# Two PSUM banks in turn for the row maxima and three for the exponentials, in an attention and FP4 feed-forward kernel

## The reference, cut to what matters

```
xn = layernorm(x)
q = rope((xn @ Wqa @ Wqb).reshape(b, s, 16, 8))
k, v = (xn @ Wkva @ Wkvb).reshape(b, s, 4, 8, 2)[..., 0], [..., 1];  k = rope(k)
scores = einsum('bqhd,bkhd->bhqk', q, k) * 8 ** -0.5, causal
attn = softmax(scores) @ v @ Wout + bout
h = silu(fp4(xn) @ fp4(w_gate).T) * (fp4(xn) @ fp4(w_up).T)
out = x + attn + fp4(h) @ fp4(w_down).T
```

## Time and profile before

| | |
|---|---|
| median of 3 runs | 816.93 us (815.31 to 818.28) |
| the profiled execution, its own time | 814.38 us |
| its span, first to last instruction | 812.6 us |
| busy share of PE, DVE, POOL, ACT | 91%, 78%, 75%, 68% |
| mean granted TensorE clock | 0.985 of full speed |
| DMA, mean | 72 GB/s |

### The profile page before, as it was taken

The page is one execution under the profiler, slowest core; times in us unless marked ns, Lnnn a source line. Parts: engine busy times, 40 slices in busy tenths (PEclk is TensorE's granted clock), DMA queues, the critical chain, the costliest instruction groups (busy, mean ns, idle before and its releaser), DMA issues.

```text
span 812.6 us, 18664 instructions
## 1 busy us (share of the span) xinstructions
PE 742.4 (91%) x6641; PEld 465.3 (57%) x6733; DVE 636.3 (78%) x1394; ACT 554.2 (68%) x1170; POOL 606.1 (75%) x707
## 2 busy tenths in 40 slices
PE   2376999999999999999999999999999999999986
PEld 1233555665656566665656566665656566665544
DVE  5569888888788888888788888888788888877511
ACT  1212677777777777777777777777777777677672
POOL 5533697878788797878788797878788797856662
PEclk9977899999999999999999999999999999999999
DMA  4423232141414233241414232141414232240000
GB/s 113 122 55 103 55 97 59 57 114 47 100 33 111 54 97 73 66 105 46 101 34 110 55 103 68 57 114 46 102 35 107 54 94 63 59 99 3 28 8 20
DMA packets 66518, 58.24 MB, mean 72 GB/s; under 512 B 17554, under 2 KB 56434, under 8 KB 66426
## 3 DMA queue, kind: packets, MB, share of 16 engines
q1 hardware_dynamic: 66426, 57.04, 27.4%
HBM read 31.81 MB, written 18.61 MB: 62 GB/s over the span
## 4 chain that ended last, share of the span: by engine, by line
PE 73%; DVE 8%; ACT 6%; POOL 5%; issue 3%; SPq 2%; DMA 2%; another core or an unknown queue 0%; POOLq 0%; DVEq 0%; ACTq 0%
PE pv_ps L1057 18%; PE max_ps L1021 12%; PE exp_ps L1036 11%; PE misc_ps L1073 6%; PE max_ps L1022 6%; PE misc_ps L1122 5%; DVE neg_max L662 4%; PE misc_ps L1081 3%; PE misc_ps L1100 3%; ACT P L854 2%; PE misc_ps L1120 2%; PE misc_ps L1110 2%; PE misc_ps L1090 1%; POOL P L478 1%; PE misc_ps L1077 1%
## 5 line engine op out<-in xcount | busy, mean ns | idle before, releaser
L662 DVE TENSOR_REDUCE neg_max<-max_ps 128x1 f32<-128x512 f32 (+3 forms) x768 | 433.4, 594 | 110.3 <-PE max_ps L1022 108.7
L854 ACT ACTIVATE P<-exp_ps 128x512 f32<-128x512 f32 x512 | 293.5, 596 | 176.8 <-remote 95.7
L1021 PE MATMUL max_ps<-K,Q 128*128 128x384 bf16 (+2 forms) x768 | 199.7, 279 | 24.6 <-DMA Kd<-K 10.9
L1036 PE MATMUL exp_ps<-Q,K 128*128 128x384 bf16 (+3 forms) x932 | 208.4, 292 | 7.5 <-ACT P L854 6.0
L1022 PE MATMUL max_ps<-Kd,Q 128*128 128x128 bf16 x1024 | 190.7, 221 | 1.5 <-DVE neg_max L662 1.5
L478 POOL TENSOR_SCALAR_AFFINE_SELECT P<-P 128x512 f32<-128x512 f32 x256 | 161.6, 667 | 32.6 <-ACT P L857 32.6
L1057 PE MATMUL pv_ps<-P,V 128*32 128x512 f32 (+3 forms) x2048 | 164.2, 439 | 1.2 <-POOL P L478 0.8
L1021 PEld LDWEIGHTS max_ps<-K,Q 128*128 128x128 bf16 x768 | 75.2, 100 | 96.0 <-DVE neg_max L662 42.7
L1022 PEld LDWEIGHTS max_ps<-Kd,Q 128*128 128x128 bf16 x1024 | 99.4, 99 | 42.6 <-issue 22.8
L510 POOL TENSOR_TENSOR h<-gate_sb,up_half 128x352 f32<-128x352 f32 x64 | 59.6, 932 | 62.4 <-DVE gate_sb L675 62.3
L1036 PEld LDWEIGHTS exp_ps<-Q,K 128*128 128x128 bf16 x1024 | 82.3, 98 | 37.0 <-ACT P L854 14.2
(11 more groups left out here) (113 smaller groups left out, 1024.0 us busy)
## 6 DMA issues: line engine op xcount, KB each, us to landing
Q<-q_scr SPq DMA_DIRECT2D x64, 224.0 KB
q_scr<-q_split SPq DMA_DIRECT2D x16, 384.0 KB, 2.6
Kd<-K SPq DMA_DIRECT2D x64, 96.0 KB
x_in<-x SPq DMA_DIRECT2D x16, 256.0 KB, 5.3
q_scr<-q_split SPq DMA_DIRECT2D x16, 256.0 KB, 2.9
x_res<-x SPq DMA_DIRECT2D x16, 256.0 KB, 5.8
out<-y SPq DMA_DIRECT2D x32, 128.0 KB, 3.1
K<-k_scr SPq DMA_DIRECT2D x64, 48.0 KB
```

The lines of the kernel that those rows point to most:

```text
L662: nc.vector.tensor_reduce(neg_max[:, pr // 4, i, heads[0]:heads[0] + len(heads), pr % 4], max_ps[r % 3][:, 0:len(heads) * n].rearrange("p ...
L854: nc.scalar.activation(P[g % 2][:, hh + r % 2, col:col + 512], ps[:, :], ACT.Exp, scale=SCALE).then_inc(exp_done, 1)
L1021: nc.tensor.matmul(ps[:, col:col + d], Qt, Kt[:, half, g, 0:d], start=True, stop=True)
L1036: last = nc.tensor.matmul(exp_ps[n % 2][:, col:col + width], K[par][:, half, pr // 2, kb * 128:(kb + 1) * 128], Q[par][:, pr, kb * 128:S], ...
```

## The change

One bank moves from the maxima to the exponentials. The maximum tiles use two banks in turn (`r % 2`; there are six tiles per pair, so the turn stays even across pairs) and the wait of PE before tile r is now for the reduction of the tile two places before. The exp tiles use three banks in turn, counted over all batches since 40 tiles per batch is no multiple of three, and the wait of PE before an exp tile is for ACT's reading of the tile three places before. No instruction is added, removed or put elsewhere on any engine.

```diff
-        max_ps = [... (f"max_ps{i}", [128, 512], F32)) for i in range(3)]
-        exp_ps = [... (f"exp_ps{i}", [128, 512], F32)) for i in range(2)]
+        max_ps = [... (f"max_ps{i}", [128, 512], F32)) for i in range(2)]
+        exp_ps = [... (f"exp_ps{i}", [128, 512], F32)) for i in range(3)]
...
-                                        max_ps[r % 3][:, 0:len(heads) * n].rearrange("p (h k) -> p h k", k=n),
+                                        max_ps[r % 2][:, 0:len(heads) * n].rearrange("p (h k) -> p h k", k=n),
...
-                ps = exp_ps[n % 2]
+                ps = exp_ps[(T.batch(0) * NPAIR * NEXP + n) % 3]
...
-                T.wait(pe, max_read, NPAIR * NMAX, 1, pr * NMAX + r - 2)
+                T.wait(pe, max_read, NPAIR * NMAX, 1, pr * NMAX + r - 1)
...
-                Kt, ps, g, n = K[T.par(1)], max_ps[r % 3], pr // 2, (i + 1) * 128
+                Kt, ps, g, n = K[T.par(1)], max_ps[r % 2], pr // 2, (i + 1) * 128
...
-                T.wait(pe, exp_done, NPAIR * NEXP, 0, n - 1)
+                T.wait(pe, exp_done, NPAIR * NEXP, 0, n - 2)
...
-                    last = nc.tensor.matmul(exp_ps[n % 2][:, col:col + width], ...
+                    last = nc.tensor.matmul(exp_ps[(T.batch(0) * NPAIR * NEXP + n) % 3][:, col:col + width], ...
```

More of the change, by code:

```diff
@@ L218, in build @@
         hqT = sb("hqT", [128, 3, S])
-        max_ps = [ctx.enter_context(nc.psum_tensor(f"max_ps{i}", [128, 512], F32)) for i in range(3)]
-        exp_ps = [ctx.enter_context(nc.psum_tensor(f"exp_ps{i}", [128, 512], F32)) for i in range(2)]
+        max_ps = [ctx.enter_context(nc.psum_tensor(f"max_ps{i}", [128, 512], F32)) for i in range(2)]
+        exp_ps = [ctx.enter_context(nc.psum_tensor(f"exp_ps{i}", [128, 512], F32)) for i in range(3)]
         pv_ps = ctx.enter_context(nc.psum_tensor("pv_ps", [128, 512], F32))
@@ L1035, in exp_tile @@
                     width = S - kb * 128
-                    last = nc.tensor.matmul(exp_ps[n % 2][:, col:col + width], K[par][:, half, pr // 2, kb * 128:(kb + 1) * 128],
+                    last = nc.tensor.matmul(exp_ps[(T.batch(0) * NPAIR * NEXP + n) % 3][:, col:col + width], K[par][:, half, pr // 2, kb * 128:(kb + 1) * 128],
                                             Q[par][:, pr, kb * 128:S], start=True, stop=True)
```

## The result

| | before | after |
|---|---|---|
| median | 816.84 us (815.31 to 818.28, 4 runs) | 842.56 us (841.69 to 844.79, 4 runs) |
| ratio, 95% interval | | 1.032 (1.030 to 1.035) |
| the profiled execution, its own time / span | 814.38 / 812.6 us | 841.69 / 839.9 us |

The change makes the kernel 3.2% slower. 847 was forecast, with 826 to 862 as the range.

A forecast was written before the change was run, and what follows sets the result against it. PE was taken to bound the kernel, its delays paid in 15 full iterations: 31.7 + 2 (iteration -1) - 4 (tail) = +29.7 us on the profiled 814.38, 844.1; with the median 2.55 above that execution, 847 us, range 826 to 862.

The forecast's parts named there:

- What bounds the kernel: Full iterations: PE busy 44.86 of 45.69 us; a PE delay is paid 15 times unless PE stood still later for something fixed.
- six places: Per full iteration, delays in slots 4 (0.89), 7 (0.67), 1 (0.12), 2 (0.16), 5 (0.13) and 6 (0.14 us).
- stricter wait: PE's wait before a maximum tile, now for a reduction one place later; to cost 2.11 us per full iteration.
- 15 times the sum: The 15 iterations with both maxima and exponentials: 2.11 us lost in each, +31.7 us.
- looser wait: PE's wait before an exp tile, now for an ACT reading one place earlier; to gain 0 in the 15 full iterations.
- Iteration -1: Iteration with maxima but no exponentials: +2 us, ends 0 and +5; losses after 62 us hidden under the DMA chain.
- The tail: After the last maxima: third exp bank lets PE reach the product with V earlier; -4 us, ends -1 and -8.
- The granted clock: Full iterations: PE clock to stay 1.00 despite new pauses; rival, a fall to 0.83, about 987 us, chance 0.04.
- They swallow: Rival: new pauses shrink PE's old waits for `o_norm` and `up_half`, leaving 0.87 us per iteration; 828 us, chance 0.10.
- Only the largest: Rival: DVE catches up fully, so an iteration loses only slot 4's 0.89 us; 827 us, chance 0.09.
- They add: Rival: slot 4's shortfalls stand side by side, 3.30 us in place of 0.89; 883 us, chance 0.07.
- Faster: Rival: pauses are covered by queued matmuls, so the tail decides at -4 us; 813 us, chance 0.03.

## Why the prediction was right

- **What bounds the kernel.** Right. In iterations 1 to 13 the PE's delays were paid at every one of the six places, with 0.13 given back behind slot 7 and 0.04 in slot 5, and nothing but the stricter wait was needed for them.
- **The stricter wait, 2.11 us per iteration.** Measured 1.88. Five of the six places came out within 0.02 of the forecast, slot 4 with its give-back among them. The term that was off is slot 7: 0.67 forecast, 0.57 - 0.13 measured. DVE's x_scale had taken 0.27 in the kernel before, where it started while POOL's addition was running, and takes 0.17 now, which is the 0.10. The 0.13 is given back at the transpositions of h and the product with V behind them, which had short gaps of their own; I had let only tile 4 of slot 4 give anything back.
- **15 times the sum, +31.7.** Measured +26.8: 24.4 for 13 iterations, 0.8 for iteration 0 and 1.6 for iteration 14. These two were taken as full, and were not. In iteration 14 it is the term for the looser wait that failed. It was put at 0 for all 15 iterations from waits read between 148 and 676 us, which lie in iterations 1 to 13; in iteration 14 exp tiles did wait for ACT (7 times, 2.2 us). The stricter wait alone costs 2.2 us there (45.10 against 42.89), much as forecast, and the third exp bank gives back 0.65. In the kernel before, iteration 0 has 4 such waits, 1.8 us, that are gone in the changed kernel; there the runs don't separate what each of the two waits does.
- **Iteration -1, +2.** Measured +3.6, within its ends of 0 and +5. I took what comes after 62 us to be hidden under the DMA chain. In the chain of waits of the changed kernel, it is PE and DVE in turn right up to the next iteration:

```profile
79.27 0.70 DVE neg_max L662
...
80.02 0.50 PE max_ps L1021
...
80.66 1.29 DVE neg_max L662 x2
...
83.80 0.70 DVE neg_max L662
...
84.55 0.50 PE max_ps L1021
```

  With three banks the maxima of that iteration were done in time for the PE to wait for DMAs there; with two they end after the DMAs. The step that failed is the overlap: the DMA chain hides nothing once the maxima end behind it.

  The granted clock of this iteration was also lower, 0.75 where it was 0.82, but that is not the 3.6 us: with the stricter wait alone in the kernel before, the clock is 0.84 and the iteration takes 40.9 us all the same. The iteration in the kernel before, in the changed kernel, and with the stricter wait alone:

```profile
43.93:81.21 37.28, 27.87 (x168) 15.05 (x169) 32.87 (x75) 8.90 (x20) 15.07 (x21) 0.82 0.28 74
```
```profile
43.67:84.55 40.88, 30.46 (x168) 15.93 (x169) 33.59 (x75) 8.80 (x20) 15.21 (x21) 0.75 0.25 69
```
```profile
44.14:85.03 40.89, 29.48 (x168) 15.64 (x169) 33.80 (x75) 8.91 (x20) 15.15 (x21) 0.84 0.26 71
```

- **The tail, -4.** Measured -3.0. The third bank saves up to one exponential in most slots, as supposed: by the first exp tile of slot 7 the tail is 3.9 ahead. Then 1.0 is given back at the first transposition of h, which waits for POOL's last quantization step. That step ends at 818.88 + 2.60 = 821.48, and the weight load and the matmul of the transposition follow:

```profile
818.88 2.60 POOL L494 TENSOR_TENSOR h<-h,h_scale 128x1408 f32<-128x1408 f32 x1
...
821.59 0.42 PEld L1100 LDWEIGHTS misc_ps<-ident,h 128*128 128x128 f32 x4 [1.03 <-issue]
...
821.62 0.63 PE L1100 MATMUL misc_ps<-ident,h 128*128 128x128 f32 x4 [0.82 <-POOL h L494]
```

  I had named POOL as what could hold the PE in the tail, and left the size open.
- **The sum.** The parts make +27.3 us on the span of the profiled executions, where +29.7 was forecast. That the difference is so small is in part luck: 4.9 us too much in the iterations 0 to 14 stand against 1.6 too little in iteration -1 and 1.0 too much gain in the tail.
- **The granted clock.** As forecast it stays at 1.00 in iterations 1 to 13, and on to the end of the span, with a pause of 1.1 us in each iteration. The rule named ahead (the Trainium skill, TensorE: Matmul & The Clock Gate, section "A second HAM failure mode: psum-queue depth-cycling") did not come to bear here.
- **The rivals.** "They swallow" is out: from 148 to 676 us the waits for `o_norm` and `up_half` are as long as before (9.9 us in 12 waits and 4.6 in 11, where it was 9.1 in 11 and 4.5 in 11). "Only the largest" is out: all six pauses are there. "They add" is out: slot 4 costs 0.87, not 3.30. "Faster" needed the pauses to be covered by queued matmuls; five of the six moved the matmuls' starts by what was forecast, within 0.02 us, and slot 7 by 0.44. Two of their prices were not worked out like the rest: "only the largest" took the tail at -5 in place of -4, which gave 827 where -4 gives 828, and "faster" left out the +2 of iteration -1 and what slot 4 might cost.

## What to carry to other kernels

How many buffers a ring needs is not told by the consumer's mean rate (DVE was busy 85% of the iteration before) but by the longest stretch of other work between two of its reads: compare, tile by tile, the end of the read two or three places back with the start of the producer, and sum what is negative, giving back only at places where the producer already waits for the same thing. Read it in every phase: here the first and the last iteration of the 15 behaved otherwise than the 13 between them. Where such a stretch is short of a buffer, moving the consumer's other work by a tile or two can be worth most of the buffer (here 20.2 of 25.7 us, though the same move also takes 5.0 us off the kernel that has the buffer). A buffer that pays in one phase can be lent in that phase: a bank idle in the tail gave the 3.0 us that the third exp bank gains there, at no cost.

## What the runs showed of the hardware

The DVE operations `h_mag` and `x_scale`, whose one input lies in SBUF, wait for POOL's operations. `h_mag` (1408 elements) takes 0.52 us alone and 0.99 beside four causal operations. A 32-element x_scale takes 0.17 alone and 0.60 when it starts while POOL's 1.28 us addition is running, and then ends 0.04 behind it. POOL waits in its turn. Of the four causal operations of slot 4, in the kernel before, the second starts just ahead of the first `h_mag` operation (425.69 to 426.68) and takes its usual time, and the third starts while that operation is there:

```profile
425.67 0.64 POOL L478 TENSOR_SCALAR_AFFINE_SELECT P<-P 128x512 f32<-128x512 f32 x1
...
426.25 0.92 POOL L478 TENSOR_SCALAR_AFFINE_SELECT P<-P 128x512 f32<-128x512 f32 x1
```

The reductions out of PSUM wait for nothing of the kind: in the changed kernel, from 148 to 676 us, the median is 0.69 us for one of 512 columns and 0.55 for one of 384, beside POOL's work and where POOL is idle alike. The Trainium skill, SBUF — State Buffer, section "SBUF: two separate sides", says that DVE in a mode with two ports and GpSimd take a shared pair of ports in turn, for a whole instruction each. The rows agree with that, though no run shows in which mode the two operations ran. I had read 0.99 and 0.84 as the price of the operation itself, when over half a microsecond of the pause that they cause is the neighbour's.
